# Two half-chunks of the shared expert behind attention, squares of 1024 columns, V scaled on GpSimd, and a new order of instructions

## What is computed

```python
# attention: 16 query heads of 64, 8 heads of K and V, each shared by 2 query heads
q, k = rope(q), rope(k)
s = einsum('bthd,bshd->bhts', q, k) / 8
logits = 2 * log(abs(s) + 1e-30) + log_G[t] - log_G[s]      # log_G: cumulated forget gates
a = where(causal, exp(logits - rowmax), 0)                   # = s**2 * decay, scaled
y = (a @ v) / (a.sum() + 1e-6)
y = (y - mean(y)) / sqrt(var(y) + 1e-9) * ln_w
attn = y.reshape(...) @ w_proj
# experts: h = layernorm(xn) * ln_g + ln_b over 4096 tokens
routed = top-2 of 7 experts, capacity 366, 128 -> 512 -> 128, weighted by gates
shared = silu(h @ W1s) * (h @ W3s) @ W2s
out = x + attn + routed + shared
```

## Time and profile before

| | us |
|---|---|
| median of three runs (lowest, highest) | 1081.27 (1080.37, 1083.77) |
| profiled execution, its own time | 1083.86 |
| its span, first to last instruction | 1082.1 |
| PE, DVE, ACT, POOL busy | 946.3, 809.5, 686.5, 604.6 |
| mean granted TensorE clock | 0.946 |

### The profile page before, as it was taken

One profiled execution on the slowest core, in us unless ns is written; L12 is line 12 of the kernel. 1 busy time (PEld: TensorE's weight loads), 2 busy tenths in 40 slices (PEclk: granted clock), 3 DMA queues, 4 the chain that ended last, 5 costly groups with the idle time before them and its releaser, 6 DMA issues.

```text
span 1082.1 us, 22031 instructions
## 1 busy us (share of the span) xinstructions
PE 946.3 (87%) x8487; PEld 667.2 (62%) x8487; DVE 809.5 (75%) x1503; ACT 686.5 (63%) x1141; POOL 604.6 (56%) x520
## 2 busy tenths in 40 slices
PE   4999989979788898989998989898998989898952
PEld 3675566657565666666765656665766666666642
DVE  5678648877888787869686868777777878685962
ACT  2343358757566675767687677777768768677730
POOL 0311429666666786556565574757466556566341
PEclk9999999998999898989998989999999999998986
DMA  9301213242524243423624352634252444434127
GB/s 258 89 1 45 54 46 89 70 105 49 117 55 104 66 107 89 105 68 69 134 56 98 89 103 65 139 70 105 77 128 52 112 95 90 108 67 95 34 46 199
DMA packets 92792, 96.00 MB, mean 89 GB/s; under 512 B 26605, under 2 KB 77677, under 8 KB 92560
## 3 DMA queue, kind: packets, MB, share of 16 engines
q1 hardware_dynamic: 87616, 91.92, 36.0%
q0 software_dynamic: 5072, 2.67, 1.9%
HBM read 49.47 MB, written 14.50 MB: 59 GB/s over the span
## 4 chain that ended last, share of the span: by engine, by line
PE 52%; DMA 17%; ACT 10%; SPq 9%; DVE 7%; issue 3%; POOL 1%; POOLq 0%; ACTq 0%; DVEq 0%
PE PS L570 16%; PE PS L748 14%; PE PS L778 11%; DMA Kt<-Kt 8%; DMA U<-H_d 6%; ACT U L924 5%; SPq L499 4%; SPq L448 3%; PE PS L613 2%; PE PS L616 2%; PE PS L623 2%; DMA SQ<-R_d 2%; ACT AX L924 1%; ACT U L850 1%; PE PS L697 1%
## 5 line engine op out<-in xcount | busy, mean ns | idle before, releaser
L748 PE MATMUL PS<-Qt,Kt 64*128 64x256 f32 (+1 forms) x2560 | 322.7, 400 | 67.3 <-DMA Kt<-Kt 41.1
L748 PEld LDWEIGHTS PS<-Qt,Kt 64*128 64x128 f32 x2560 | 258.5, 208 | 124.2 <-issue 34.3
L924 ACT ACTIVATE U<-PS,ESG,ES 128x512 f32<-128x512 f32 x288 | 207.1, 791 | 116.0 <-PE PS L748 113.0
L778 PE MATMUL PS<-U 128*64 128x256 f32 (+1 forms) x1920 | 202.3, 358 | 7.8 <-POOL U L1473 4.7
L1462 POOL TENSOR_TENSOR U<-U,consts 128x512 f32<-128x512 f32 x96 | 128.5, 1339 | 100.9 <-DMA U<-U 100.7
L778 PEld LDWEIGHTS PS<-U 128*64 128x64 f32 x1920 | 133.1, 137 | 77.9 <-issue 9.7
L1343 DVE TENSOR_TENSOR PS<-U 128x512 f32<-128x512 f32 x64 | 75.2, 1175 | 72.8 <-POOL U L1473 63.0
L1473 POOL TENSOR_TENSOR U<-U 128x768 f32<-128x768 f32 x41 | 76.1, 1855 | 73.4 <-ACT U L913 73.3
L1523 POOL TENSOR_TENSOR U<-U,SQ 128x1024 f32<-128x1024 f32 x32 | 77.2, 2412 | 60.7 <-DMA SQ<-R_d 60.6
L1479 POOL TENSOR_SCALAR_AFFINE_SELECT U<-U 128x256 f32<-128x256 f32 x128 | 56.2, 441 | 90.4 <-ACT U L850 89.8
L1349 DVE TENSOR_TENSOR PS<-U,PS 128x512 f32<-128x512 f32 x144 | 99.9, 694 | 7.5
(11 more groups left out here) (181 smaller groups left out, 1456.7 us busy)
## 6 DMA issues: line engine op xcount, KB each, us to landing
U<-U SPq DMA_DIRECT2D x192, 128.0 KB
U<-H_d SPq DMA_DIRECT2D x32, 512.0 KB, 5.3
SQ<-R_d SPq DMA_DIRECT2D x64, 256.0 KB, 6.5
Kt<-Kt SPq DMA_DIRECT2D x32, 256.0 KB, 9.4
U<-in_w SPq DMA_DIRECT2D x21, 256.0 KB, 4.5
acc<-in_x SPq DMA_DIRECT2D x4, 512.0 KB, 5.7
ye_d<-SQ SPq DMA_DIRECT2D x4, 512.0 KB, 7.8
R_d<-U SPq DMA_DIRECT2D x16, 128.0 KB
```

Source lines behind the costliest of these rows:

```text
L748: mm = te.matmul(bank[:, 256 * n:256 * n + 256 - lo], Kt[u % 2][(ki + hd) % 2][rows, 128 * j:128 * j + 128], Qt[p % 2][m // 2][rows, 256 * ...
L778: mm = te.matmul(P[4][64 * hd:64 * hd + 64, c + lo:c + 256], vt, A[s % NA][:, o:o + 256 - lo], start=begins and n == 0, stop=ends and n == 1)
L924: sq = s.activation(A[n % NA].rearrange("p (a n t) -> p n a t", a=2, n=2)[:, t], PS[:, first:first + 1024].rearrange("p (a n t) -> p n a t ...
```

## The change

It has six parts.

1. Half-chunks 6 and 7 of the shared expert (`NT = 2`, `NSH = 6`) leave the set-up. Their normalised tokens stay in `HX`; `sload` reads the weights again in pair 31, and the products (`sup`: sixteen on TensorE, eight silus on ScalarE, eight multiplications on VectorE) and the two down products (`sdn`) run behind the last values. The last store waits for them.
2. An off-diagonal step is squared by one instruction of 1024 columns with a constant scale and bias. `ESG` and its two VectorE instructions go.
3. The column factor goes into V: `scale_values` (`vs`) on GpSimd writes `VS` for the units with off-diagonal steps, three products per pair, and off-diagonal value products read `VS`. It waits for the last value product that read the buffer before. `ES` holds the square of the factor it held.
4. `maximum` multiplies by the factor as it takes the maximum (scalar_tensor_tensor). The unit without off-diagonal steps is reduced straight from `A` in two pieces.
5. Unit 1 of even pairs, and of pair 31, is light.
6. All tables have new numbers.

```diff
-HEAVY = [(3,)] * 9 + [(1, 3)] * 23
+NT = 2
+NSH = 8 - NT
+HEAVY = [(3,)] * 9 + [(3,), (1, 3)] * 11 + [(3,)]
-SP_AT = [..., (-21.66, 'keys', 0), (-22.28, 'row', 0), (-20.51, 'weights', 0), ...]
+SP_AT = [(-2.14, 'sload', 0), ..., (-22.71, 'keys', 0), (-22.72, 'row', 0), (-12.55, 'weights', 0), ...]
...
-                    for t, j in enumerate(blocks):
-                        c = ES_AT[m] + 16 * m * (p // 8) + KVH * j + p % 8
-                        sq = s.activation(A[n % NA].rearrange("p (a n t) -> p n a t", a=2, n=2)[:, t],
-                                          PS[:, first:first + 1024].rearrange("p (a n t) -> p n a t", a=2, n=2)[:, t],
-                                          ACT.Square, scale=ES[:, c:c + 1], bias=ESG[:, c:c + 1])
-                    sq.then_inc(a_so, 1)
+                    s.activation(A[n % NA], PS[:, first:first + 1024], ACT.Square, scale=0.125,
+                                 bias=GUARD).then_inc(a_so, 1)
...
+            def scale_values(p, w):
+                u, hu, m = p // 2, p % 2, ORDER[w]
+                c = ES_AT[m] + 16 * m * (p // 8) + p % 8
+                po.wait_ge(a_es, 1)
+                po.wait_ge(a_v, 2 * u + (2 * m - 1) // 4 + 1)
+                if p:
+                    po.wait_ge(p_av, 10 * (p - 1) + taken_of(w, True)[-1] + 1)
+                else:
+                    po.wait_ge(v_gt, 4 * NSH)
+                g.tensor_tensor(VS[m].rearrange("p (j d) -> p j d", d=64),
+                                Vt[u % 2].rearrange("p (k n d) -> p k n d", k=NB, d=64)[:, 0:2 * m, hu],
+                                bc(ES[:, c:c + 16 * m - 7:8], 2, 64), ALU.mult).then_inc(g_vs, 1)
...
-                    pe.wait_ge(a_v, 2 * u + (2 * m - 1) // 4 + 1)
+                    pe.wait_ge(g_vs, 3 * p + w)
...
-                    a4 = A[s % NA].rearrange("p (a n t) -> p a n t", a=2, n=4)
-                    v.tensor_tensor(RUN.rearrange("p (a n t) -> p a n t", a=2, n=2), a4[:, :, 0:2], a4[:, :, 0:3:2],
-                                    ALU.max).then_inc(v_mx, 1)
-                    fold(un)
...
+                    v.tensor_reduce(MR[:, c:c + 16].rearrange("p (a b) -> p a b", a=2), a4[:, :, 0:8], AX, ALU.max,
+                                    apply_transpose=True).then_inc(v_mt, 1)
...
+                    v.tensor_reduce(MT.rearrange("p (a b) -> p a b", a=2), a4[:, :, 8:12], AX, ALU.max,
+                                    apply_transpose=True).then_inc(v_mx, 1)
...
+                    v.tensor_tensor(hi, hi, MT.rearrange("p (a b) -> p a b", a=2), ALU.max).then_inc(v_red, 1)
...
+                        v.scalar_tensor_tensor(run if i == m and n == 1 else PRUN, a_[:, :, n], es, PRUN, ALU.mult,
+                                               ALU.max).then_inc(v_mx, 1)
...
+                elif kind == "sup":
+                    pe.wait_ge(s_tw, 48)
+                    te.matmul(pb[:, :], TW[w][:, 128 * f:128 * f + 128], HX[c], start=True, stop=True).then_inc(p_su, 1)
```

More of the change, by code:

```diff
@@ L64 @@
 SP_FIRST = [("row", 0), ("swapk", 0), ("swapq", 0), ("keys", 0)]
[L65 removed]
+SP_AT = [(-2.14, 'sload', 0), (14.27, 'tops', 0), (24.68, 'rows', 0), (-26.04, 'swapk', 0), (-25.19, 'swapq', 0), (-22.71, 'keys', 0), (-22.72, 'row', 0), (-12.55, 'weights', 0), (-8.35, 'weights', 1), (34.76, 'roots', 0), (36.55, 'spread', 0)]
 LOAD_AT = [20 * EXPERT_PAIRS[-1] + 76 + b for b in range(B)]
@@ L276, in block_program @@
         wpr = take(1024)
-        take = carve(6912)
+        take = carve(7168)
         XC = [take(1024) for _ in range(2)]
@@ L286, in block_program, with hidden @@
         wv_ = take(512)
+        def hidden(half):
+            return HX[half - NSH] if half >= NSH else hT[:, 512 * half:512 * half + 512]
         hn_v = hn.rearrange("p (k c) -> p k c", c=HS)
```

179 lines of the change are left out of this document (120 added, 59 removed), and 7 rows, old and new, of tables (ACT_FIRST, PE_FIRST).

## The result

| | median, us | runs (lowest to highest) | profiled span, us |
|---|---|---|---|
| before | 1080.82 | 4 (1078.47 to 1083.77) | 1082.1 |
| after | 1105.97 | 4 (1104.92 to 1106.93) | 1103.9 |

The ratio is 1.0224, 95% interval [1.0183, 1.0265]. The kernel is 25 us slower (24 by the ratio), where the record said 1057 and at most 1078.

A forecast was written before the change was run, and what follows sets the result against it. TensorE's work (busy 87%) plus its idling, mainly on key transfers and ScalarE's squares, bounds the kernel. Squares -26, scaled V +12, copies -4, front -12, tail +6 sum to -24 us: 1057 us, range 1026 to 1078.

The forecast's parts named there:

- Squares: Off-diagonal score steps: one 1024-column square of 1.04 us frees ScalarE and shortens TensorE's waits, -26 us (-17 to -48).
- V scaled by GpSimd: GpSimd's queue in attention: a V product ahead of the query rotation makes odd pairs' scores late, +12 us (0 to +35).
- A sign of being wrong: Attention: the forecast is wrong if TensorE waits over 1 us per pair for scaled V or Qt.
- Maxima and VectorE: VectorE's maxima take in the factor; the engine, 75% busy and mostly ahead, adds nothing: 0 us (-5 to +8).
- Rival (c): Gain eaten by VectorE's first scales in even pairs, or squares gain nothing: 1072 to 1085 us, chance 0.12.
- Rival (b): GpSimd becomes the bound through values, scaled V, rotation, scores; slower, at about 1095 us, chance 0.1.
- Keys first: SyncE's queue: the order still puts root spreading and decay row ahead of the key copies, so 0 us.
- the hole: In every duo, TensorE waits for a 10 to 12 us key or decay-row transfer: 41.1 us in 14 waits.
- rival (d): Keys not copied first; had they been, about 1016 us; chance 0.03 that a shift elsewhere does it.
- Front: Set-up's end: two half-chunks leave, so first scores start at about 132 instead of 143.73, -12 us (-6 to -22).
- tail: Behind the last values: moved expert products delay the sums of squares and roots, +6 us (+1 to +14).
- Copies to Y: Copies one place earlier and fewer GpSimd products ahead of values: a small gain, -4 us (-10 to 0).

The follow-up runs named there:

- e3: Kernel after with the old HEAVY list and the third unit's scaling back ahead of the first unit's maximum: 1082.23 us, ratio 1.0047.
- e9: e3 with GpSimd's V products for units 1 and 2 placed directly behind the query rotations they stood ahead of: 1066.07 us, ratio 0.9879.
- e12: e9 with the key copies issued ahead of the decay row in every duo: 1065.60 us, ratio 0.9880.
- e15: e9 with no half-chunk moved, all eight ahead of attention in the old set-up order: 1073.92 us, ratio 0.9971.
- e10: e9 with the last duo's sums of squares ahead of the first moved down product, VectorE's moved work behind the roots: 1064.23 us, ratio 0.9864.
- e7: Kernel before with only the squares made one 1024-column instruction with constants, key factors left out: 1063.10 us, ratio 0.9835.

## Why the prediction was wrong, point by point

- **Squares, -26 (-17 to -48).** Mechanism and duration right (1.036 us, taken 1.04), the size at its lower end: -18 alone (-10 to -26). ScalarE was freed of 83 us and not of 102 (the squares' busy time went from 276 to 193), since successive squares overlapped by some 0.1 us in before. That part of the weight loads' waits only hid the next wait is an argument; no run shows it.
- **V scaled by GpSimd, +12 (0 to +35).** The loop was named rightly (values, product, rotation, scores), its size wasn't: 30 us, 18 of them by place. The products themselves were taken too long: they are 65 us in all in the kernel after, not 79. The record weighed only the 128-column product in the odd pairs and wrote that in an even pair the key copy hides it. The 256-column product stands ahead of the first query rotation in the same way; the record didn't cost it. A sign of being wrong that it had named came about: the weight loads of the scores waited 29.8 us for Qt in 216 to 1026 us, some 1 us per pair (17.7 in before). A second part came unforeseen: in e3 the first half of the roots was stretched. Its operations L1438, L1442, L1448 and L1450 sum to 22.1 us for 9 duos in e3, to 9.5 for 10 in e9. How the 18 us divide between the two wasn't tried.
- **Maxima and VectorE, "mostly ahead; it is no part of the sum", 0 (-5 to +8).** This is the step that failed outside its own range. The argument was VectorE's share, 75% of the span. The light units' 12 x 0.947 were counted on VectorE and priced at nothing; they cost 19 to 24 us, since they stand ahead of the roots. Without them (e3) the kernel is 5 us above before and not 24; the forecast's gain of 24 is missing there mostly for two other terms, V's 18 over and the squares' 8 under. The maximum itself came out within the record's 90 ns: L1407 takes 753 ns where L1349 took 694, for its new form and the factor from memory together.
- **Rival (c)** had VectorE's first scales, 1 us per duo, but in the even pairs, where the chain starts with the key landing and the roots don't follow. The slip on the parity hid the place where a query swap, the roots and the scales meet. The true price is 1.6 to 2 us for each light pair. The rival had 0.12 and an end at 1085.
- **Rival (b)**, GpSimd the bound at 1095, had a time near the right one, but the loop it named gives 30 us and the 36 it needed for the sign weren't reached: with HEAVY of before even the tight loop leaves 1082.
- **Keys first, 0.** Right: not done, and the hole stayed (29.8 us in 11 waits). But rival (d) gave 1016 if it were done, and e12 did it: nothing. The sum of a wait isn't what its removal gives.
- **Front, -12, and tail, +6.** Right: the first scores start 11.3 earlier and the tail is 6.5 longer by the trace (the sums ended 16.6 us behind the values, for 18.4). The -2.4 for the decay factors and the +1.7 for the clock weren't isolated. The move of the two half-chunks is worth 10 us in e15 against e9, 4 of them in the middle.
- **Copies to Y, -4.** No run isolates it.
- **The sum with measured terms**: squares -18, products +30, move of the half-chunks -10, HEAVY and scale 2 +19: +21. Measured are +24 (0.0224); each term carries some 5 to 9 us, and the terms are not quite additive (HEAVY is 19 with GpSimd's loop and 24 without).

Still open: whether e10's tail is worth its 5 us in the time, and whether the roots' second half ahead of the *first* scale would give e9 another microsecond per duo. It wasn't tried.

## What to carry to other kernels

Price a moved or added operation by what stands behind it in its own queue, not by the engine's share: follow each thing that the engine hands on (here small roots to a queue of DMA issues) to where it closes a loop, and note how many microseconds of slack the loop has before adding one. When a large gain is made on one engine (the squares), the slack of others can shrink by it (from 1.6 to 0.9 us per duo in e7), and an edit that was free before can then cost more than it moves. And when the kernel after is slower, undo one table or list at a time before doubting the idea: with two products and one scale moved and the old list HEAVY it runs in 1066.07 us (ratio 0.9879 [0.9848, 0.9910]), faster than both.
